# Local attention: where the mask is added to the scores

## What is computed

```python
mask = (it < jb) | (it > jb + w) | (jb == -1)
sim = jnp.einsum('bhwie,bhwje->bhwij', bq, bk2) * QK_SCALE
sim = jnp.where(mask, -jnp.finfo(sim.dtype).max, sim)
attn = jax.nn.softmax(sim, -1)
out = jnp.einsum('bhwij,bhwje->bhwie', attn, bv2)
```

## Time and profile before

| | us |
|---|---|
| median of 3 runs | 4736.38 |
| lowest and highest run | 4717.23 and 4738.95 |
| profiled execution | 4727.04 |
| its span in the trace | 4725.3 |
| PE, VectorE, ACT, POOL busy | 3968.6, 2877.1, 2199.4, 1806.5 |

### The profile page before, as it was taken

How to read it: one execution, slowest core, us unless ns; L and a number is a source line. 1 busy time by engine, 2 the same in 40 slices (tenths; PEclk the granted TensorE clock), 3 DMA queues, 4 the chain that set the end, 5 groups by cost and what they waited for, 6 DMA issues and landing times. The chain is left out here.

```text
span 4725.3 us, 99085 instructions
## 1 busy us (share of the span) xinstructions
PE 3968.6 (84%) x37576; PEld 3122.0 (66%) x37576; DVE 2877.1 (61%) x4358; ACT 2199.4 (47%) x4317; POOL 1806.5 (38%) x1571
## 2 busy tenths in 40 slices
PE   4666689899899899899899848989988976667998
PEld 1224468778678688678678638888888863225555
DVE  6894657367367367367377276665556544985554
ACT  4442267467467467467467423333323223442222
POOL 2560067257157167167167133323333311552000
PEclk7997789999999999999999969999888787897999
DMA  0000011011011011011011000000000000001000
GB/s 13 0 0 16 6 49 34 24 37 33 22 37 34 22 39 32 22 39 34 19 41 32 5 5 4 4 3 2 4 4 4 2 5 6 0 0 54 0 0 9
DMA packets 56469, 81.92 MB, mean 17 GB/s; under 512 B 13146, under 2 KB 32628, under 8 KB 54900
## 3 DMA queue, kind: packets, MB, share of 16 engines
q1 hardware_dynamic: 56052, 75.99, 5.4%
HBM read 30.87 MB, written 1.05 MB: 7 GB/s over the span
## 5 line engine op out<-in xcount | busy, mean ns | idle before, releaser
L1622 POOL TENSOR_TENSOR local_rot<-local_term 128x512 f32<-128x512 f32 x384 | 478.3, 1266 | 640.3 <-DVE local_term L1940 640.3
L1940 DVE TENSOR_TENSOR local_term<-bank,local_table 128x512 f32<-128x512 f32 x768 | 484.5, 673 | 107.7 <-ACT local_sq L1828 99.2
L1863 ACT ACTIVATE local_attn<-bank 64x256 f32<-64x256 f32 x768 | 290.7, 378 | 340.7 <-PE bank L1719 333.8
L1113 POOL TENSOR_TENSOR delta_lt_n<-delta_lt,delta_joint 128x512 f32<-128x512 f32 x224 | 289.4, 1322 | 409.6 <-PE bank L1198 252.2
L272 POOL TENSOR_TENSOR mamba_hc<-mamba_state,mamba_c_all 128x512 f32<-128x512 f32 x256 | 319.5, 1270 | 312.4 <-DVE mamba_state L451 308.1
L1628 POOL TENSOR_TENSOR local_rot<-local_rot,local_inv 128x512 f32<-128x512 f32 x384 | 392.2, 1042 | 91.8 <-ACT local_inv L1839 90.3
L1663 PE MATMUL bank<-local_w_layer,local_xs 128*128 128x256 f32 x1536 | 400.9, 406 | 25.6 <-issue 19.4
L1663 PEld LDWEIGHTS bank<-local_w_layer,local_xs 128*128 128x128 f32 x1536 | 287.8, 197 | 79.4 <-issue 29.6
L2001 DVE TENSOR_REDUCE local_most<-bank 128x8 f32<-128x512 f32 x192 | 132.8, 692 | 311.5 <-PE bank L1698 311.5
L1399 DVE TENSOR_TENSOR delta_x_all<-delta_x_all,bank 128x512 f32<-128x512 f32 x160 | 109.8, 686 | 337.8 <-PE bank L1208 337.8
L1719 PE MATMUL bank<-local_pt,local_v_moved 64*128 64x64 f32 x3072 | 314.7, 282 | 0.0
(11 more groups left out here) (349 smaller groups left out, 9125.6 us busy)
## 6 DMA issues: line engine op xcount, KB each, us to landing
local_v_moved<-local_v_at SPq DMA_DIRECT2D x192, 192.0 KB, 2.4
local_w_layer<-a_w_layer_dram SPq DMA_DIRECT2D x6, 1536.0 KB, 6.9
local_v_moved<-local_v_at SPq DMA_DIRECT2D x192, 32.0 KB, 2.0
moe_w<-f_w_dram SPq DMA_DIRECT2D x3, 2048.0 KB, 16.3
local_w_o<-a_w_o_dram SPq DMA_DIRECT2D x12, 256.0 KB, 3.9
local_w_up<-a_w_up_dram SPq DMA_DIRECT2D x6, 341.0 KB, 4.2
moe_w<-f_w_dram SPq DMA_DIRECT2D x3, 576.0 KB, 5.9
delta_w_h<-g_w_qkv_dram SPq DMA_DIRECT2D x8, 192.0 KB, 2.3
```

Source lines behind the costliest of these rows:

```text
L1113: pool.tensor_tensor(lt_n[:, lv % 2, n, :, :], lt[:, n, :, :], joint[:, lv, :].unsqueeze(1).to_broadcast([P, QUAD, C]), ALU.mult).then_inc ...
L1622: pool.tensor_tensor(rot[:, i % 2, :, f, :], here[:, :, f, :], there[:, :, 1 - f, :], ALU.add).then_inc(summed, 1)
L1863: ins = act.activation(tokens[ch, v, :, :].rearrange("p k (r q) -> p k r q", r=2), g.bank[6 + v][ch, :].rearrange("p (k r h q) -> p k r h ...
L1940: dve.tensor_tensor(term[:, which, b, :], g.bank[b][:, :], table[:, which, :, :].rearrange("p n c -> p (n c)"), ALU.mult).then_inc(roped, 1)
```

## The change

The matmul that opened the bank with the mask is gone, with the bf16 identity. The first score matmul into each region of the bank has `start=True` in its place. The mask is held in float32, and VectorE adds it to the scores as it moves them from the bank into `z`; the maximum and the subtraction then read `z`. A new semaphore `masked` counts the addition; VectorE waits for it ahead of the maximum, and PE waits for it, in place of `z_ready`, before it writes the bank again.

```diff
--- before.py
+++ after.py
@@ -1497,8 +1497,7 @@
         v_at, v_moved = sb("v_at", [P, TILES, P]), sb("v_moved", [P, TILES, P])
         attn = sb("attn", [P, PAIRS, N])
         sq, lg = sb("sq", [P, 2, GROUP]), sb("lg", [P, 2, GROUP])
-        mask = sb("mask", [P, 2 * TPG, 2 * W], BF16)
-        ident_b = sb("ident_b", [P, P], BF16)
+        mask = sb("mask", [P, 2 * TPG, 2 * W])
         z = sb("z", [P, 2, GROUP])
         term = sb("term", [P, 2, SPG, GROUP])
         rot = sb("rot", [P, 2, TPG * 4, 2, W])
@@ -1519,7 +1518,7 @@
         v_ready, v_used, v_shifted = sem("v_ready"), sem("v_used"), sem("v_shifted")
         sums_ready, inv_ready, normalized = sem("sums_ready"), sem("inv_ready"), sem("normalized")
         q_turned, k_turned, q_copied, k_copied = sem("q_turned"), sem("k_turned"), sem("q_copied"), sem("k_copied")
-        s_ready, z_ready, e_ready = sem("s_ready"), sem("z_ready"), sem("e_ready")
+        s_ready, masked, z_ready, e_ready = sem("s_ready"), sem("masked"), sem("z_ready"), sem("e_ready")
         total_ready, p_ready = sem("total_ready"), sem("p_ready")
         pt_ready, pt_copied, o_ready, o_copied, wo_ready = (
             sem("pt_ready"), sem("pt_copied"), sem("o_ready"), sem("o_copied"), sem("wo_ready"))
@@ -1611,7 +1610,6 @@
                                             pattern=[[0, 2 * TPG], [-1, 2 * W]], channel_multiplier=1))
             for first in (0, TPG):
                 own.step(pool.memset(mask[0:H * W, first, 0:W], -1e30))
-            own.step(pool.tensor_copy(ident_b[:, :], g.ident[:, :]))
             pool.sem_inc(made, 1)
 
             def add_turned(s, i):
@@ -1682,9 +1680,7 @@
                     mm.then_inc(signal, 1)
 
             def score(s, i):
-                pe.wait_ge(z_ready, s + 1)
-                pe.matmul(S_BANK[:, :], ident_b[:, :], mask[:, :, :].rearrange("p x k -> p (x k)"),
-                          start=True, stop=True, skip_group_check=True)
+                pe.wait_ge(masked, s + 1)
                 pe.wait_ge(q_copied, s + 2)
                 wait_apart(pe, k_copied, s + 2, pe_passed)
                 for b in range(SPG):
@@ -1696,7 +1692,7 @@
                                 query = b * T + w * W
                                 row = H * W * r + W * hh
                                 mm = pe.matmul(S_BANK[row:row + W, column:column + 2 * W], q_rot[ch, i % 2, query:query + W],
-                                               k_rot[ch, i % 2, b, w * W:(w + 2) * W], start=False, stop=True, skip_group_check=True)
+                                               k_rot[ch, i % 2, b, w * W:(w + 2) * W], start=True, stop=True, skip_group_check=True)
                 mm.then_inc(s_ready, 1)
 
             def turn_probs(s, i):
@@ -1927,7 +1923,7 @@
         @block.vector
         def _(dve):
             dve.wait_ge(made, 1)
-            for free, n in ((vecs_free, 1), (tabled, 1), (xr_ready, 4), (roped, 4), (z_ready, 1), (sums_ready, 1)):
+            for free, n in ((vecs_free, 1), (tabled, 1), (xr_ready, 4), (roped, 4), (masked, 1), (z_ready, 1), (sums_ready, 1)):
                 dve.sem_inc(free, n)
             STEPS = 2
 
@@ -1998,8 +1994,10 @@
                     most_of, sums, over = most[:, i % 2, :], total[:, i % 2, 0, :], total[:, i % 2, 1, :]
                     dve.wait_ge(s_ready, s + 1)
                     scores = S_BANK[:, :].rearrange("p (x k) -> p x k", k=2 * W)
-                    own.step(dve.tensor_reduce(most_of, scores, AX.X, ALU.max))
-                    dve.tensor_tensor(rows, scores, spread(most_of, 2 * W), ALU.subtract).then_inc(z_ready, 1)
+                    dve.tensor_tensor(rows, scores, mask[:, :, :], ALU.add).then_inc(masked, 1)
+                    dve.wait_ge(masked, s + 2)
+                    own.step(dve.tensor_reduce(most_of, rows, AX.X, ALU.max))
+                    dve.tensor_tensor(rows, rows, spread(most_of, 2 * W), ALU.subtract).then_inc(z_ready, 1)
                     if ahead:
                         rope(s + 2, 0, 0)
                     dve.wait_ge(e_ready, s + 1)
```

## The result

The changed kernel is slower: 4818.98 us in the median of 4 runs (4816.55 to 4831.43) against 4737.66 (4717.23 to 4740.01). The ratio is 1.0187, with a 95% interval of 1.0153 to 1.0220. The forecast was 4815 us. The profiled execution took 4817.81 us, its span is 4815.8 us.

A forecast was written before the change was run, and what follows sets the result against it. It took a loop over PE, ACT's copies and POOL's multiplies to set the 7.55 us slot; 180 x 0.45 = +81 us, with -2 from last slots, gave +79: 4815 us against 4736, 8-in-10 range 4775 to 4850.

The forecast's parts named there:

- The slot and its loop: Local stage: PE's transposes and value matmuls, ACT's copies and POOL's two multiplies form the loop setting the 7.55 us slot.
- PE's own pause: Before the query/key transposes L1681: PE's weight loads stand still 0.15 us, waiting for POOL's multiplies.
- The mask matmul, 0.22 us of PE's time: Removed from PE in each slot: scores come 0.22 us earlier, worth nothing on the path that sets the slot.
- the last slot of a layer: PE alone is on the path there; removing the mask matmul saves 0.3 us, 6 times, -2 us.
- The added pass: VectorE, score bank plus mask to SBUF, once per slot: 0.69 us, covered.
- POOL's room: Between the end of POOL's additions L1622 and the next multiplies L1628; later VectorE work uses 0.26 us, leaving 0.23.
- The collision: Subtraction with two SBUF inputs takes turns with POOL's two multiplies: second multiply ends 0.45 us later per slot.
- How many slots: Slots where subtraction and multiplies meet: 30 in each of 6 layers, 180, from slot 2 on, not slot 32; +81 us.
- Rival 1: POOL keeps its turn and VectorE's subtraction loses: 0.52 us a slot, 180 times, 4828 us; chance 0.17.
- Rivals 2 and 3: 2: nothing collides, 4734 us, chance 0.13; 3: PE sets the slot, 0.22 us less each, 4694 us, chance 0.05.
- rival 4: A full turn each, blocked side starting from nothing: second multiply 0.73 us late per slot, 4865 us; chance 0.07.

The follow-up runs named there:

- no mask: The kernel before without the mask matmul and nothing in its place, so attention is unmasked; ratio 1.0003, slot 7.55 us.
- norms between the copies: The kernel before, with ACT making the inverse norms between the second and third of its four output copies; 4718.90 us, ratio 0.9960.
- the maxima in the bank: The changed kernel with the eight maxima per partition written to the score bank, PE waiting for the subtraction again; 4738.05 us, ratio 0.9999.
- the last run: The changed kernel as it is, with ACT making the inverse norms between the second and third output copy; 4803.00 us, ratio 1.0154.
- both masks: The changed kernel with the mask matmul kept as well, from a bf16 copy of the mask; 4825.10 us, ratio 1.0177.

## Why the prediction was right

- *The slot and its loop.* Shown: the transposes wait for POOL's multiplies, PE's own relief leaves the slot at 7.55 us (no mask), and ACT's part of the loop, made shorter, shortens the slot (norms between the copies).
- *PE's own pause.* Read as 0.15 us from the loads. In the matmuls it was 0.10, as the norms between the copies showed. It changes nothing in the forecast, since POOL sets the slot either way.
- *The mask matmul, 0.22 us of PE's time.* The pause grew from 0.15 to 0.37 us in the run without a mask. In the last slot of a layer I took 0.3 us. PE's timeline of one such slot, first before and then after the change:

```profile
1565.62 1.12 PE L1706 MATMUL bank<-ident,local_z 128*128 128x128 f32 x4
...
1568.95 7.69 PE L1732 MATMUL bank<-local_w_o,local_attn 128*128 128x128 f32 x64
```

```profile
1604.90 1.12 PE L1702 MATMUL bank<-ident,local_z 128*128 128x128 f32 x4
1605.94 1.93 PE L1694 MATMUL bank<-local_k_rot,local_q_rot 64*32 64x64 f32 x64
...
1607.81 7.86 PE L1728 MATMUL bank<-local_w_o,local_attn 128*128 128x128 f32 x64
```

From the transposes to the output projection it is 2.91 us instead of 3.33, so 0.4 us less, in each of the six layers. In the total it can't be seen: what lies between one layer's transposes of slot 32 and the next layer's first ones, and behind the sixth, came out 1.7 us longer in all (689.6 against 687.9).

- *The added pass.* Foreseen at 0.69 us and covered; 692 ns measured, and covered (the maxima in the bank). Of POOL's room 0.27 us went, 0.26 foreseen. The maximum over SBUF took 0.69 instead of 0.68.
- *The collision.* Foreseen: subtraction at 0.90 us, first multiply unchanged, second at 1.49, slot 8.00. Measured: 0.90, 1.04, 1.49, 8.00. The mean of the multiplies is 1254 ns, foreseen 1.25 us. That the two SBUF operands are the cause is shown by two runs that move one of them, each in its own way, and in both the cost is gone.
- *How many slots.* 30 a layer were foreseen, from slot 2 on. The subtractions of slots 1 and 2 in the third layer of the changed kernel:

```profile
1357.48 0.69 DVE L2000 TENSOR_TENSOR local_z<-local_z,local_most 128x512 f32<-128x512 f32 x1
...
1365.06 1.19 DVE L2000 TENSOR_TENSOR local_z<-local_z,local_most 128x512 f32<-128x512 f32 x1
```

  In slot 32 it takes 0.69 us again. Slot 2 has two forms. In the first and third layer the subtraction is the longer one (1.39 and 1.19 us). In the other four it issues 0.03 to 0.04 us ahead of the first multiply and keeps 0.69 us, and that multiply takes 1.56. So all 180 pairs meet, but four of them in the other order. From the first transposes of a layer to those of its slot 32 the six layers together took 1409.1 us before and 1490.4 after: 81.3 us, where 180 x 0.45 = 81 was foreseen.
- *The rivals.* Rival 1 does not happen in the change, but in the last run. Rivals 2 and 3 fell with the slot of 8.00 us, rival 4 with the 0.55 and 0.90 us. The Trainium skill's rule ("SBUF — State Buffer", section "Who interferes with whom") holds here in who blocks whom. The blocked subtraction, though, ended 0.55 us behind the multiply and not its whole 0.69 us, and the blocked multiply 0.90 us behind and not 1.04.

What the prediction did not have is that the stages behind move by themselves. Between the last addition of the local stage and the end, the kernel before took 2004.8 us and the changed one 2014.4. Over the 14 profiled executions of this study this untouched part took between 2001.5 and 2030.9 us, and by and large the longer it took, the more of it had been granted to PE at the half clock (1.2 GHz): 513 us in the shortest, 584 in the longest, a mean granted clock of 0.87 and 0.86. Why a program falls on one or the other stays open. That the forecast came within 4 us of the median is therefore partly luck. The slot and its 81 us were foreseen, and the movement of 29 us behind them was not.

## What to carry to other kernels

Ahead of every edit that moves an operand of VectorE from the bank to SBUF, look at what GpSimd does at that moment. Here an elementwise instruction with two SBUF inputs took turns with GpSimd's multiplies, and both lost: 0.69 us became 0.90, or up to 1.51 with the norms between the copies, and 1.04 became 1.49. A single small operand kept in PSUM was enough to avoid it (687 ns, and the whole 81 us back). And a pause of PE that its busy share hides can be read from its weight loads: 0.15 us of it told that PE's relief would be worth nothing.

If one order of waits is exchanged for another on a queue, ask what stands behind the moved wait; splitting the work so that the wait falls where its data is due gave two versions faster than both kernels. They are the kernel before (4718.90 us, 0.4% under it) and the change with the maxima in the bank (4709.62 us, 0.6% under), both with the norms between the copies. Which of the two is faster these runs don't decide: the intervals of their ratios overlap.

## What was not expected of the hardware

- A VectorE operation issued 0.12 us before POOL's ended was not lengthened at all (both masks). By the differences, the part that needs no turn is 0.13 to 0.14 us on both engines: 0.69 - 0.55, 1.04 - 0.90 and, in the delta stage, 1.27 - 1.14.
- The sum of the exponents took 676 ns in the median before (L2006) and 686 ns in the change (L2004), with the same operands. It costs nothing here, and its cause was not tried.
